# Edge counting in a GNN and FFN kernel: one comparison for the one-hots of six groups, interleaved, and staging three windows ahead

## The reference

```python
    e = e_left[src] + e_right[dst]
    e = jnp.where(e >= 0, e, NEG_SLOPE * e)
    e_max = segment_max(e, dst, num_segments=N)
    e_exp = jnp.exp(e - e_max[dst])
    denom = segment_sum(e_exp, dst, num_segments=N)
    alpha = e_exp / (denom[dst] + EPS)
    out = segment_sum(Wh[src] * alpha[:, :, None], dst, num_segments=N)
```

## Time and profile before

| | us |
|---|---|
| median of 3 runs (lowest, highest) | 4386.68 (4383.18, 4397.35) |
| profiled execution, its own time | 4381.9 |
| its span | 4380.3 |
| first one-hot to last `combine` of the counting | 58.24 to 687.78 |

### The profile page before, as it was taken

One profiled execution on the slowest core, in us unless ns is written; L12 is line 12 of the kernel. 1 busy time (PEld: TensorE's weight loads), 2 busy tenths in 40 slices (PEclk: granted clock), 3 DMA queues, 4 the chain that ended last, 5 costly groups with the idle time before them and its releaser, 6 DMA issues. The chain is left out here.

```text
span 4380.3 us, 72251 instructions
## 1 busy us (share of the span) xinstructions
PE 3495.6 (80%) x25428; PEld 2519.0 (58%) x25429; DVE 3066.7 (70%) x4546; ACT 2200.6 (50%) x3295; POOL 215.8 (5%) x212
## 2 busy tenths in 40 slices
PE   3555554688888868888883799949996999799799
PEld 1222223466666646666662466548885888688677
DVE  6888986799999879999985222255544554555456
ACT  2444441788888868888880111114442444244322
POOL 0000000000000000000000244400000000000010
PEclk8656666899999989999995899969998999899889
DMA  1111112311111031111103722233313330333220
GB/s 44 62 63 70 61 64 55 120 64 62 58 53 63 33 121 62 62 63 47 63 33 122 252 46 46 41 124 120 114 57 122 117 117 30 136 117 117 73 66 30
DMA packets 135678, 347.31 MB, mean 79 GB/s; under 512 B 28337, under 2 KB 106423, under 8 KB 117847
## 3 DMA queue, kind: packets, MB, share of 16 engines
q1 hardware_dynamic: 114240, 313.75, 20.3%
q0 software_dynamic: 13888, 20.07, 2.5%
q10 hardware_dynamic: 7254, 9.67, 0.6%
HBM read 278.31 MB, written 65.14 MB: 78 GB/s over the span
## 5 line engine op out<-in xcount | busy, mean ns | idle before, releaser
L817 ACT ACTIVATE a_probsT<-a_psT 128x896 f32<-128x896 f32 (+1 forms) x1100 | 900.6, 836 | 765.5 <-PE a_psT L938 763.1
L938 PE MATMUL a_psT<-ident,a_scores 128*128 128x128 f32 (+1 forms) x6875 | 1009.3, 286 | 134.0 <-ACT a_scores L809 117.5
L859 DVE SCALAR_TENSOR_TENSOR a_scores<-a_el,hx 128x3136 f32<-128x3136 f32 x275 | 956.7, 3479 | 91.9 <-DMA a_mask<-mask_dram 65.4
L938 PEld LDWEIGHTS a_psT<-ident,a_scores 128*128 128x128 f32 (+1 forms) x6875 | 770.5, 143 | 336.9 <-issue 193.5
L863 DVE CUSTOM_DVE_ANT_0 a_scores<-a_scores,a_mask 128x3136 f32<-128x3136 f32 x275 | 940.5, 3420 | 11.8
L809 ACT ACTIVATE a_scores<-a_scores,a_negmax 128x1664 f32<-128x1664 f32 (+1 forms) x550 | 879.1, 1598 | 43.7 <-DVE a_negmax L863 43.7
L957 PE MATMUL a_psO<-hx,a_probsT 128*128 128x256 f32 (+1 forms) x3750 | 874.8, 381 | 0.0
L957 PEld LDWEIGHTS a_psO<-hx,a_probsT 128*128 128x128 f32 (+1 forms) x3750 | 680.2, 189 | 107.3 <-issue 25.7
L954 PE MATMUL a_psO<-a_probsT,hx 128*32 128x128 f32 (+1 forms) x10000 | 586.3, 287 | 118.9 <-ACT a_probsT L817 116.1
L356 PE MATMUL cnt<-onehot_c,onehot_dst_a 128*128 128x392 bf16 x1200 | 363.9, 463 | 305.5 <-DVE onehot_c L294 256.4
L954 PEld LDWEIGHTS a_psO<-a_probsT,hx 128*32 128x32 f32 (+1 forms) x10000 | 324.2, 110 | 319.9 <-ACT a_probsT L817 171.6
(11 more groups left out here) (239 smaller groups left out, 2484.8 us busy)
## 6 DMA issues: line engine op xcount, KB each, us to landing
a_mask<-mask_dram SPq DMA_DIRECT2D x125, 1568.0 KB, 6.7
mask_dram<-logc SPq DMA_DIRECT2D x200, 196.0 KB, 1.9
moe_w<-in_L_ffn_w SPq DMA_DIRECT2D x48, 512.0 KB
a_el<-el_dram ACTq DMA_DIRECT2D x6, 1568.0 KB, 15.5
a_el<-el_dram SPq DMA_DIRECT2D x5, 1568.0 KB, 6.5
x<-n_x SPq DMA_DIRECT2D x2, 3072.0 KB
n_x<-in_x SPq DMA_DIRECT2D x8, 640.0 KB, 7.3
n_x<-x SPq DMA_DIRECT2D x8, 640.0 KB, 6.3
```

The lines of the kernel that those rows point to most:

```text
L817: nc.scalar.activation(pT[:, gi % 2, 0:w], psT[gi % 2][:, 0:w], ACT.Copy).then_inc(s_ev, 1)
L859: nc.vector.scalar_tensor_tensor(sc[:, c, :], el[:, k % H, 0, :], col(hx, b + k // H, D + h0 + k % H), el[:, k % H, 1, :], ALU.subtract, A ...
L938: last = nc.tensor.transpose(psT[gi % 2][0:r, t * P:(t + 1) * P], sc[:, k % 3, c0:c0 + r], g["ident"][:, :])
```

## The change

Both one-hots are stored with the six groups innermost: `ohA` goes from (six groups, 128) to (128, six groups), and `ohC` from (six groups, 392) to (392, six groups). Each is made by a single comparison of two 16-bit tensors: a ramp table in which every number stands six times, and the six staged codes, repeated over the columns. `stC` becomes float16 for that. The six comparisons with a per-partition scalar (line 294) are gone. TensorE's matmuls read group k out of the interleaved tensors, so that its operands (weights and moving data) step by six elements, 12 bytes. `AHEAD` goes from 2 to 3. The ramp tables that POOL makes once at the start grow six times.

```diff
@@ edges_phase
-            io(g["iotaP"][:, :], [[1, P]], 0, 0)
-            io(g["iotaC"][:, :], [[1, SC]], 0, 0)
+            io(g["iotaP"][:, :, :], [[1, P], [0, GROUP]], 0, 0)
+            io(g["iotaC"][:, :, :], [[1, SC], [0, GROUP]], 0, 0)
@@ adjacency_phase
-        SS, AHEAD, ROWS = 4, 2, 8
-        ohA = sb("onehot_dst_a", [P, 2, GROUP, P], BF16)
-        ohC = sb("onehot_c", [P, 2, GROUP, SC], BF16)
+        SS, AHEAD, ROWS = 4, 3, 8
+        ohA = sb("onehot_dst_a", [P, 2, P, GROUP], BF16)
+        ohC = sb("onehot_c", [P, 2, SC, GROUP], BF16)
...
-        stC = sb("stage_c", [P, SS, GROUP])
+        stC = sb("stage_c", [P, SS, GROUP], F16)
...
-                nc.vector.tensor_tensor(oa, g["iotaP"][:, :].rearrange("p (o n) -> p o n", o=1).broadcast_to([P, GROUP, P]),
-                                        code.rearrange("p (k o) -> p k o", o=1).broadcast_to([P, GROUP, P]), ALU.is_equal)
-                for k in range(GROUP):
-                    last = nc.vector.tensor_scalar(oc[:, k, :], g["iotaC"][:, :], c[:, k:k + 1], None, ALU.is_equal)
-                return last
+                nc.vector.tensor_tensor(oa, g["iotaP"][:, :, :],
+                                        code.rearrange("p (o k) -> p o k", o=1).broadcast_to([P, P, GROUP]), ALU.is_equal)
+                return nc.vector.tensor_tensor(oc, g["iotaC"][:, :, :],
+                                               c.rearrange("p (o k) -> p o k", o=1).broadcast_to([P, SC, GROUP]), ALU.is_equal)
...
                     for k in range(GROUP):
-                        last = nc.tensor.matmul(o, ohA[:, s, k, :], ohC[:, s, k, :], start=k == 0 and not further,
+                        last = nc.tensor.matmul(o, ohA[:, s, :, k], ohC[:, s, :, k], start=k == 0 and not further,
                                                 stop=True, skip_group_check=True)
```

More of the change, by code:

```diff
@@ L7 @@
 BF16 = mybir.dt.bfloat16
+F16 = mybir.dt.float16
 I32 = mybir.dt.int32
@@ L245, in adjacency_phase @@
         sem = lambda n: new_semaphore(nc, g, n)
-        SS, AHEAD, ROWS = 4, 2, 8
-        ohA = sb("onehot_dst_a", [P, 2, GROUP, P], BF16)
-        ohC = sb("onehot_c", [P, 2, GROUP, SC], BF16)
-        exA = sb("extra_dst_a", [P, GROUP, P], BF16)
-        exC = sb("extra_c", [P, GROUP, SC], BF16)
+        SS, AHEAD, ROWS = 4, 3, 8
+        ohA = sb("onehot_dst_a", [P, 2, P, GROUP], BF16)
+        ohC = sb("onehot_c", [P, 2, SC, GROUP], BF16)
+        exA = sb("extra_dst_a", [P, P, GROUP], BF16)
+        exC = sb("extra_c", [P, SC, GROUP], BF16)
         zA = sb("zero_a", [P, P], BF16)
@@ L254, in adjacency_phase @@
         stA = sb("stage_dst_a", [P, SS, GROUP], BF16)
-        stC = sb("stage_c", [P, SS, GROUP])
+        stC = sb("stage_c", [P, SS, GROUP], F16)
         sxA = sb("extra_stage_dst_a", [P, GROUP], BF16)
-        sxC = sb("extra_stage_c", [P, GROUP])
+        sxC = sb("extra_stage_c", [P, GROUP], F16)
         logc = sb("logc", [P, ROWS, SC])
@@ L308, in further_groups @@
                         dve.wait_ge(s_xst, i + n0 + 1)
-                        onehots(exA[:, :, :], exC, sxA[:, :], sxC).then_inc(s_xoh, 1)
+                        onehots(exA[:, :, :], exC[:, :, :], sxA[:, :], sxC[:, :]).then_inc(s_xoh, 1)
             def combine(b, j):
@@ L324, in windows @@
                     dve.wait_ge(s_used, w + 1)
-                    onehots(ohA[:, s, :, :], ohC[:, s], stA[:, j % SS, :], stC[:, j % SS]).then_inc(s_oh, 1)
+                    onehots(ohA[:, s, :, :], ohC[:, s, :, :], stA[:, j % SS, :], stC[:, j % SS, :]).then_inc(s_oh, 1)
                     if j >= 2:
@@ L350, in windows @@
                                 for k in range(GROUP):
-                                    last = nc.tensor.matmul(o, exA[:, k, :], exC[:, k, :], start=False, stop=True,
+                                    last = nc.tensor.matmul(o, exA[:, :, k], exC[:, :, k], start=False, stop=True,
                                                             skip_group_check=True)
@@ L1580, in program @@
             sbe = lambda n, s, d=F32: early.enter_context(nc.sbuf_tensor(n, s, d))
-            g["iotaP"] = sbe("iotaP", [P, P], BF16)
-            g["iotaC"] = sbe("iotaC", [P, SC], mybir.dt.float16)
+            g["iotaP"] = sbe("iotaP", [P, P, GROUP], BF16)
+            g["iotaC"] = sbe("iotaC", [P, SC, GROUP], F16)
             g["codes"] = sbe("codes", [P, 2, ECOL])
```

## The result

The changed kernel takes 4430.58 us (4429.34 to 4432.35, four runs) against 4386.35 before. The ratio, estimated over all runs, is 1.0097, with a 95% interval of 1.0079 to 1.0115. It is 44 us slower, where 4250 was forecast, 136 us faster. Its profiled execution took 4431.06 us, 49.2 more than that of before.

A forecast was written before the change was run, and what follows sets the result against it. VectorE was taken to bound the counting at 2.73 us per window. Comparisons 94 plus staging 40.3 less 3 at run starts gave 131 us off 4381.9, so 4250; forecast 4235 to 4275, wider range 4235 to 4430 (about 0.82).

The forecast's parts named there:

- What bounds the kernel: Counting stage, 629.5 us: VectorE sets the pace at 2.73 us per window; the rest is waits.
- The comparisons: VectorE's one-hots at 0.52 ns per element: 1.30 us for `ohC`, 0.48 for `ohA`, window 2.26 us, saving 94 us.
- Staging three ahead: Counting stage: with codes staged three windows ahead, VectorE's 40.3 us of waits for them vanish.
- The wait for the one-hot buffer at the starts of the runs: Two-deep buffer makes the third window wait for TensorE: 0.6 us, five times, 3 us lost.
- TensorE's operands: Matmul reads in 12-byte steps were charged nothing: six matmuls stay at 2.12 us at the lower clock.
- the rival on TensorE's reads: TensorE's stepped reads set the pace, slower than before; break-even 2.93 us per window, up to 4516 us; chance 0.16.
- "upper bound": Stepped matmul reads cost at most 0.25 us more each: window 3.60 us at the lower clock, 2.64 at the higher.
- the milder part of this rival: The milder third of the slow TensorE case, taken into the range up to 4430 us.
- POOL's ramps: At the start, larger ramp tables cost POOL 3.0 us more, done at about 8.2 us, hidden with 1.4 us of cover.
- The sum: Whole kernel: 94 + 40.3 - 3 = 131 us saved from 4381.9, so 4250 us.

The follow-up runs named there:

- the version with pairs: Changed kernel, but one-hots stored group after group as before, each code staged twice, comparisons over pairs of columns: 4242.54 us, ratio 0.9663 to the kernel before.
- the probe: Kernel before plus a leading stage of TensorE matmuls on zeros, each series with another operand step: 0.17 to 0.70 us per matmul; whole program 4538.72 us.

## Why the prediction was wrong, step by step

**What bounds the kernel** was read rightly. VectorE set the pace: 0.49 us off its window (2.73 to 2.24 in the version with pairs) is 98 us, the staging alone is worth 45 to 49, and the version with both is 147 us faster than the kernel before.

**The comparisons** were right in every number: 1.38 against 1377 ns, 0.56 against 558 ns. Between the two that is 819 ns for 1584 elements, 0.52 each. The doubled rate holds for two 16-bit tensors with unit steps, with the codes read again every six elements or every two. Of the 0.49 us, 0.39 come from `ohA` (0.87 to 0.48); `ohC` goes only from 1.38 to 1.30, as its comparisons with a scalar were fast already, and the version that kept them (stepped weights alone) is only 20 us behind the one with pairs.

**Staging three ahead** was right: 40 promised, 45 measured by itself in the stage and 49 in the time. The wait for the one-hot buffer at the starts of the runs was right too, 3.1 us against 3.

**TensorE's operands** is the step that failed: "Twelve bytes are far closer to the contiguous end, and I take nothing." A matmul that moves 392 columns in 12-byte steps takes 0.522 us, not 0.33 or less. Six make 3.13 us, above VectorE's 2.24 and above the 2.93 that the rival on TensorE's reads gave as its point of no gain, and the stage lasts 200 x 3.13 + 44 = 670 us. Two things were wrong in the reasoning. Distance in bytes was taken as a scale with 128 bytes at its end, while the cost saturates at 16 bytes: of the full price, 12 bytes cost three quarters. And the price was put on top of the column time at either clock (3.60 and 2.64 us per window), while by the probe it stands in its place: the longer of the two counts, so a window would take 3.13 at either level. With that the "upper bound" at the higher clock, 2.64, was none; it came from VectorE's read of a 128-byte step and could not bound another engine. The rival that was given a chance of 0.16 had the engine and the sign; its time of 4516 was too high. The measured 4430.6 lies beside the upper end of the stated range, 4430, by accident: that end was drawn to take in the milder part of this rival and rests on no window of 3.13 us.

The Trainium skill had spoken for that rival ("Advanced Engine Details and Errata", "SBUF Cachelines"): 16-byte lines, and at least two hits in each to hide the memory's latency. It gives no price. The probe agrees at 16-byte granularity; at 8 bytes, where every line still gets two hits, a matmul at the higher clock already takes 0.35 us instead of 0.17, so for TensorE the rule is too mild.

**POOL's ramps** failed as well, at 7.1 us: "3.0 us more; ... Hidden, with 1.4 us of cover." Their price per element was taken from a ramp in one run of 392 (1.15 ns), while runs of six equal numbers cost 7.41 / 2352 = 3.15 ns, so GpSimd was busy until 14.4 us and not 8.2. And the cover was reckoned against TensorE's first transposes, while the victim was VectorE's conversion at 7.9 us, which needs nothing that the ramps make.

The sum as it should have stood: 40.5 us from 200 windows of 3.13, 7.1 from the start, against 49.2 measured between the two executions; the other 1.6 us lie behind the stage (from its end to the end of the span it is 3694.2 us, where it was 3692.5) and were not traced further. One small slip in the prediction changes nothing here: a window of 2.85 us gives 4365 by its own sum, not 4368.

## What to carry to other kernels

A layout that makes one engine faster is read by another: before interleaving, price the reader's step in time per 16-byte stretch, 1.78 ns here for TensorE's moving operand, and compare it with the engine that set the pace. To get the doubled rate out of a comparison of 16-bit data with broadcast values (0.52 ns per element here, where `ohA` had 1.03), a run of two equal values was enough, so duplicate the small operand and leave the large one as its reader wants it. Work moved to GpSimd is not always free for VectorE: here one conversion waited for it and delayed everything behind it by 7 us.

## What the runs showed of the hardware that was not expected

- TensorE's moving operand in steps: 0.17, 0.17, 0.26, 0.35, 0.43, 0.52, 0.69, 0.68, 0.70 us per matmul of 392 bf16 columns at steps of 2, 4, 6, 8, 10, 12, 16, 24 and 32 bytes; the steps up to 10 bytes were taken at 1.00 of the clock, those from 16 on at 0.50; 12 bytes cost the same at both, and so do 16 bytes, by the float32 series. Weights in steps of 2, 6 and 16 elements: no change, 2.82 us for 16 matmuls.
- In that probe the clock fell to the lower level although the records show TensorE busy without a gap, in series of stepped matmuls, and it was back at 1.00 by 85 us, in the contiguous series behind them; in the changed kernel, with 12-byte steps as well but data that are not all zero, it stayed at 1.00 through the stage. What decides it was not tried.
- GpSimd's ramps of repeated numbers: 1.15 ns per element in one run of 392, 3.15 with runs of six, 4.35 / 784 = 5.5 with runs of two (the version with two groups interleaved). A VectorE conversion of 0.6 us beside them took up to 7.49, and ended 0.56 to 0.58 us after the ramp in all three programs looked at.
